# Reordering a graph layer: input normalised team by team, flips and projection placed between the products, four flip buffers

## What is computed

```python
h = relu(layernorm(x))                       # rows of 256
hidden = h @ W + b
x = x + adj @ hidden / adj.sum(axis=0)[:, None]     # layer 0
h = relu(layernorm(x))
x = x + layer1(h, S=adj)                     # two steps:
#   A = softmax of the kept 0.9 of (Xa W1 W2)(Xa W3)^T, row by row
#   Xf = Rf Xf ; Xb = Rb Xb ; Xa = A Xa  (Rf, Rb: adj + I, divided by its row and column sums)
#   Z += Xf U1 + Xb U2 + Xa U3 ; result: layernorm(X + Z) * gamma + beta
```

## Time and profile before

| what | us |
|---|---|
| median of 3 runs | 2404.68 (2404.57 to 2407.76) |
| the profiled execution's own time | 2408.84 |
| its span, first to last instruction | 2406.6 |
| start until the main products of tile 0 (L730) | 60.0 |
| first layer, tiles 0 to 25 | about 60 to 365 |
| second norm and projections, until the first logits | about 365 to 445 |
| attention layer, two steps, and the end | about 445 to 2406.6 |

### The profile page before, as it was taken

The page is one execution under the profiler, slowest core; times in us unless marked ns, Lnnn a source line. Parts: engine busy times, 40 slices in busy tenths (PEclk is TensorE's granted clock), DMA queues, the critical chain, the costliest instruction groups (busy, mean ns, idle before and its releaser), DMA issues.

```text
span 2406.6 us, 38368 instructions
## 1 busy us (share of the span) xinstructions
PE 1959.0 (81%) x12364; PEld 1462.6 (61%) x12364; DVE 1722.7 (72%) x4419; ACT 1223.4 (51%) x1886; POOL 68.3 (3%) x115
## 2 busy tenths in 40 slices
PE   0888884479999999999656498988989898898980
PEld 0777772267777777777444166665656666565660
DVE  5111116488888888888882688888888888888866
ACT  1111113556666666666331675766657576665720
POOL 0000002100000000000000000000000000000000
PEclk9999996689999999999878699999999999999995
DMA  4555551111111111111003001001010100101003
GB/s 107 142 142 142 142 127 71 32 36 40 40 40 43 43 48 46 41 43 40 19 20 97 19 18 35 25 27 35 17 35 17 35 30 22 35 17 35 16 20 118
DMA packets 59226, 123.87 MB, mean 51 GB/s; under 512 B 13491, under 2 KB 45617, under 8 KB 58928
## 3 DMA queue, kind: packets, MB, share of 16 engines
q1 hardware_dynamic: 45872, 93.58, 11.5%
q0 software_dynamic: 3744, 22.14, 5.3%
q10 hardware_dynamic: 9568, 7.67, 1.0%
HBM read 107.99 MB, written 37.49 MB: 60 GB/s over the span
## 4 chain that ended last, share of the span: by engine, by line
DVE 34%; PE 31%; DVEq 13%; ACT 12%; issue 7%; DMA 2%; ACTq 1%; SPq 0%
DVE scraps L1064 7%; PE bank L730 7%; PE bank L817 6%; DVE stats L1194 5%; DVE window L1064 4%; PE lg L783 4%; ACT turned L600 3%; ACT turned L602 3%; DVEq L1369 3%; PE bank L826 3%; ACT expo L583 3%; PE bank L849 3%; PE bank L803 3%; DVEq L1241 2%; DVE window L1237 2%
## 5 line engine op out<-in xcount | busy, mean ns | idle before, releaser
L826 PE MATMUL bank<-xcur,probs_t 128*128 128x256 f32 x2704 | 597.4, 381 | 2.5 <-ACT probs_t L636 2.5
L826 PEld LDWEIGHTS bank<-xcur,probs_t 128*128 128x128 f32 x2704 | 509.5, 190 | 76.3 <-issue 3.3
L817 PE MATMUL bank<-ident,window 128*128 128x128 f32 x1352 | 242.3, 337 | 193.4 <-DVE kept_inv L1371 172.7
L817 PEld LDWEIGHTS bank<-ident,window 128*128 128x128 f32 x1352 | 182.3, 170 | 281.4 <-DVE kept_inv L1371 196.5
L636 ACT ACTIVATE probs_t<-bank 128x512 f32<-128x512 f32 (+1 forms) x364 | 194.9, 566 | 299.6 <-PE bank L817 297.6
L803 PE MATMUL bank<-both,s_tile 128*128 128x512 f16 x1352 | 300.1, 379 | 0.0
L1049 DVE TENSOR_SCALAR_CACHE_REDUCE expo<-lg 128x1024 f32 (+1 forms) x208 | 204.9, 1022 | 122.0 <-PE lg L783 113.3
L583 ACT ACTIVATE expo<-expo,neg_max 128x3327 f32<-128x3327 f32 x52 | 159.7, 3070 | 232.3 <-DVE neg_max L1058 232.3
L602 ACT ACTIVATE turned<-expo,found 128x3327 uint8<-128x3327 f32 x78 | 239.6, 3071 | 5.4
L600 ACT ACTIVATE turned<-expo,found 128x3327 uint8<-128x3327 f32 x78 | 239.3, 3068 | 3.7
L1194 DVE MAX8 stats<-window 128x8 f32<-128x208 f32 (+1 forms) x780 | 238.8, 384 | 0.0
(11 more groups left out here) (226 smaller groups left out, 2181.4 us busy)
## 6 DMA issues: line engine op xcount, KB each, us to landing
s_tile<-s_scratch SPq DMA_DIRECT2D x52, 832.0 KB, 4.6
s_scratch<-s_tile SPq DMA_DIRECT2D x26, 832.0 KB, 3.4
expo<-in_adj POOLq DMA_DIRECT2D x25, 831.8 KB, 7.1
x_scratch<-both SPq DMA_DIRECT2D x1, 3328.0 KB, 9.5
q_tile<-q_scratch SPq DMA_DIRECT2D x104, 32.0 KB, 3.3
xa_scratch<-ht ACTq DMA_DIRECT2D x26, 128.0 KB, 1.7
y_scratch<-y_tile ACTq DMA_DIRECT2D x26, 128.0 KB, 1.7
xcur<-xa_scratch SPq DMA_DIRECT2D x1, 3328.0 KB, 12.4
```

The costliest lines, as they stand in the source:

```text
L817: last = T.transpose(flip_ps[g % 2][:, k * P:(k + 1) * P], window[:, (k0 + k) * P:(k0 + k + 1) * P], ident[:, :])
L826: last = T.matmul(pv_ps[:, 0:D], probs_t[:, k * P:(k + 1) * P], xcur[:, k, :], start=(k == 0), stop=(k == NT - 1))
```

## The change

- **Input.** `x` is loaded by team, without waiting for `x_pad` (only the tail does). For each team VectorE makes moments, reciprocal and `-mean * rstd`; ScalarE makes the square root, one Relu with scale and bias for each tile and one copy for the high part; GpSimd makes the low part, one tile at a time, after it has issued the first two `adj` loads, and signals `low_first`. TensorE waits for `low_first` team by team inside tile 0's products.
- **First layer.** Four flip buffers instead of two (the two new ones lie in `probs_t` and `window`), and two PSUM tiles for the products (`s_ps`, `lg[1]`). The counts and flips of tile t+1 stand among tile t's products, before k = 12, 14, 18 and 21; the transposes of tile t-1 stand before k = 3 and its projection before k = 8. The hardware loop has 6 passes of four tiles. VectorE's and ScalarE's moves follow that order.
- **Weights.** W1 times W2 is made after tile 0's products.
- **Second norm.** The column counts are closed before tile 25's products. VectorE starts on the inverses and on teams 0 and 1 then; its last work for tile 25 (`with_loops`, `projected_out`) and the row and column inverses stand ahead of team 2.

```diff
+TURN_AT = 3
+PROJECT_AT = 8
+FLIP_AT = (12, 14, 18, 21)
+TEAM_STARTS = [t0 for t0, _ in TEAMS]
+        s_buf = [s_tile[0], s_tile[1]] + [home[:, c0:c0 + NP // 2].bitcast(BF16).rearrange("p (k q) -> p k q", k=NT)
+                                          for home, c0 in ((probs_t, (DC + 1) * D), (window, 0))]
+        conv_ps = [s_ps, lg[1]]
+        def at(i, j):
+            return i * 4 + j, i * 2 + j // 2, j % 2, i + j // 4, j % 4
+        def convolve_all(eng, convolve):
+            convolve(at(0, 0), at(0, 1), first=True)
+            with eng.Fori(0, NT // 4) as i:
+                for j in range(1, 5):
+                    convolve(at(i, j), at(i, j + 1))
 # SyncE
+            for g, (t0, n) in enumerate(TEAMS):
+                full = min(n, NT - 1 - t0)
+                sp.dma_start(xcur[:, t0:t0 + full, :], ...).then_inc(x_in[g], DMA)
             sp.wait_ge(x_pad, 1)
-            sp.dma_start(xcur[:, 0:NT - 1, :], ...).then_inc(x_in, DMA)
 # GpSimd
-                pool.wait_ge(x_in, DMA * 2)
-            tiles_loop(pool, load_adj)
+            pool.wait_ge(x_in[NTEAM - 2], DMA)
+            for t in range(2):
+                load_adj(t, 0, t)
+            for g, (t0, n) in enumerate(TEAMS):
+                pool.wait_ge(high_first, g + 1)
+                for t in range(t0, t0 + n):
+                    last = G.tensor_tensor(parts[:, t, 1, :], x1_all[:, t, :], parts[:, t, 0, :], ALU.subtract)
+                last.then_inc(low_first, 1)
...
 # ScalarE
+            deviation_x(0)
+            for g, (t0, n) in enumerate(TEAMS):
+                if g + 1 < NTEAM:
+                    deviation_x(g + 1)
+                act.wait_ge(norm_x, g + 1)
+                for t in range(t0, t0 + n):
+                    A.activation(x1_all[:, t, :], xcur[:, t, :], ACT.Relu, scale=rstd[:, t:t + 1], bias=mean[:, t:t + 1])
+                act.drain()
+                A.activation(parts[:, t0:t0 + n, 0, :], x1_all[:, t0:t0 + n, :], ACT.Copy).then_inc(high_first, 1)
+            for g in range(1, NA, 2):
+                move_flipped(at(0, 0), g)
+            convolve_all(act, convolve)
+            convolve(at(NT // 4, 1), None)
+            turned_out(NT - 1)
 # TensorE
+            def convolve(tile, after, first=False):
+                t, _, b, _, q = tile
                 pe.wait_ge(adj_moved_v, (t + 1) * (NA // 2) + 1)
                 pe.wait_ge(adj_moved_s, (t + 1) * (NA // 2) + 1)
-                pe.wait_ge(conv_out, t + 1)
                 for k in range(NT):
+                    if first and k in TEAM_STARTS:
+                        pe.wait_ge(low_first, TEAM_STARTS.index(k) + 1)
+                    if not first and k == TURN_AT:
+                        turn_convolved(t - 1)
+                    if not first and k == PROJECT_AT:
+                        project(t - 1)
+                    if after is not None and k == FLIP_AT[0]:
+                        count_columns(after)
+                    if after is not None and k in FLIP_AT:
+                        flip(after, FLIP_AT.index(k))
...
                 last.then_inc(conv_done, 1)
+                if first:
+                    multiply_weights()
 # VectorE
-            norm_stats(xcur)
-            stds(1)
...
+            input_moments(0)
+            for g in range(NTEAM):
+                if g + 1 < NTEAM:
+                    input_moments(g + 1)
+                input_normaliser(g)
+            def convolve(tile, after, first=False):
+                if not first:
+                    projected_out(tile[0] - 1)
+                for g in range(0, NA, 2):
+                    move_flipped(after, g)
+                with_loops(tile)
 # VectorE, second norm
             for g in range(NTEAM):
+                if g == 1:
+                    with_loops(at(NT // 4, 1))
+                    projected_out(NT - 1)
+                    dve.drain()
+                    inverse_sums()
```

More of the change, by code:

```diff
@@ L299, in graph_layers @@
         free_slots = [
-            *[(s_stored[n], DMA) for n in range(2)],
+            *[(s_stored[n], DMA) for n in range(4)],
             (adj_flipped, 8),
@@ L385, in _, with store_s @@
             load_u(0)
[L388 removed]
+            def store_s(tile):
+                t, _, _, _, q = tile
                 sp.wait_ge(s_made, t + 1)
[L390 to L391 removed]
+                sp.dma_start(dram_tile(s_dram, t), flat(s_buf[q][:, :, :])).then_inc(s_stored[q], DMA)
+            with sp.Fori(0, NT // 4) as i:
+                for j in range(4):
+                    store_s(at(i, j))
+            for j in range(NT % 4):
+                store_s(at(NT // 4, j))
             sp.wait_ge(x1_ready, 1)
@@ L504, in _ @@
         def _(act):
[L505 to L528, removed]
+            def deviation_x(g):
+                t0, n = TEAMS[g]
+                act.wait_ge(moments_x, g + 1)
+                A.activation(rstd[:, t0:t0 + n], var[:, t0:t0 + n], ACT.Sqrt).then_inc(deviations_x, 1)
@@ L711, in convolve, with flip @@
                              skip_group_check=True)
[L713 to L724, removed]
+            def flip(tile, g):
+                t, _, b, _, _ = tile
+                k0, n = ADJ_GROUPS[g]
+                pe.wait_ge(adj_moved_s if g % 2 else adj_moved_v, t * (NA // 2) + g // 2 + 1)
+                view = flip_ps[g % 2][:, :].bitcast(BF16)
+                for k in range(n):
+                    last = T.transpose(view[:, k * P:(k + 1) * P], natural[b][:, (k0 + k) * P:(k0 + k + 1) * P], ident_bf[:, :])
+                last.then_inc(adj_flipped, 1)
@@ L733, in convolve @@
                                     skip_group_check=True)
                 last.then_inc(conv_done, 1)
[L736 to L740, removed]
+                if first:
+                    multiply_weights()
+            count_columns(at(0, 0))
+            for g in range(NA):
+                flip(at(0, 0), g)
@@ new lines, in convolve @@
+            def convolve(tile, after, first=False):
+                if not first:
+                    projected_out(tile[0] - 1)
+                for g in range(0, NA, 2):
+                    move_flipped(after, g)
+                with_loops(tile)
+            for g in range(0, NA, 2):
+                move_flipped(at(0, 0), g)
+            convolve_all(dve, convolve)
+            projected_out(NT - 2)
+            dve.wait_ge(cols_done, 1)
+            V.tensor_copy(col_n[:, :], lg[0][:, 0:NT])
@@ L989, in normaliser, with result_moments @@
+            def result_moments(g):
+                t0, n = TEAMS[g]
+                for t in range(t0, t0 + n):
+                    V.scalar_tensor_tensor(out=x1_all[:, t, :], in0=x1_all[:, t, :], scalar=deg_inv[:, t:t + 1], in1=xcur[:, t, :],
+                                           op0=ALU.mult, op1=ALU.add)
+                dve.drain()
+                moments_of(x1_all, g).then_inc(moments, 1)
             def normaliser(g):
```

190 lines of the change are left out of this document (104 added, 86 removed).

## The result

The changed kernel takes 2320.66 us (median of 4, 2319.51 to 2321.97), the kernel before 2405.86 (median of 4, 2404.57 to 2407.76): ratio 0.9645, 95% interval 0.9629 to 0.9662. Forecast 2322, range 2310 to 2342. The profiled execution took 2319.51, its span is 2317.8, against 2406.6 before.

The account below looks back on a forecast made before the run. TensorE paces the loop at 11.84 us a tile and does nothing that counts until 60 us. Gains of 74.3 through tile 25 and 7.9 in the second norm, 82.2, take 2408.84 to 2326.6; median 4.2 lower: forecast 2322, range 2310 to 2342.

Parts of the forecast that it names:

- Start: Input stage: products of tile 0 start at 34.2 us instead of 60.00.
- Tile 0: First tile of the first layer, from its products to tile 1's start: 12.4 us, with ten slow steps and W1 W2.
- Tile: Steady tile of the first layer's loop: 9.85 us of TensorE work instead of 11.84, for 24 tiles 236.4.
- Tile 25: Last tile of the first layer, without flips: 7.6 us, its products ending at 290.6 instead of 364.9.
- Second norm: Products' end to the second norm's first Relu: 6.2 us instead of 14.15, a gain of 7.9.
- The handshakes: Loop waits between engines: each fits into products placed over it; for the transposes three steps, 0.73 against 0.70, stall at most 0.05.
- rival 6: Loop: adj's load misses its place, taking over 21.5 us instead of 7.1; tile 13.3, gain gone; at 22 about 2410; chance 0.01.
- the longer loop's stall: Loop's jump back: TensorE waits for code, 2 us in each of six passes, 12 us in all, 2334; chance 0.08.
- Array run-out at the switches: Loop: TensorE's array empties at switches between products and other work, 1.3 us a tile, 31 in all, 2353; chance 0.07.
- The input rival: Input stage: VectorE's small operations, stretched by GpSimd, fall behind ScalarE from team 3, 6 to 10 us, about 2330; chance 0.08.

## Why the prediction came out right

Forecast and result are 1.3 us apart. The mechanism was right, and the closeness is partly luck: two errors took most of each other back.

First, the steps against the profiled execution: 82.2 predicted, 88.8 measured in the span. *Start* 34.2 predicted, 34.8 measured (by the table above it can come nearly 3 us later). *Tile 0*: its products to tile 1's, 12.4 predicted; tile 1's transposes stand at 46.72, three steps after its first product, which is 11.2. Six steps were slow (34.80 to 37.48), where the prediction took ten by the earlier trace rows: 0.9 of the 1.2. *Tile*: 9.85 predicted, 9.65 measured; 24 tiles make 4.9 of it. Each price was right in kind and a little high (counts, transposes, flips and projection 0.68, 0.3, 1.56, 0.97 against 0.65, 0.25, 1.47, 0.94), probably because I read distances between rows with small waits between them. *Tile 25*: 7.6 and 7.5. *Second norm*: 7.9 and 8.0; the run without it cost 7.7 at that place. 1.0 more came behind it: VectorE's four operations L1064 (L971 before) of team 3 took 2.07 instead of 3.11.

Second, the profiled execution before (2408.84) lies above its median, and the one after (2319.51) is the fastest of its four; so 89.3 between profiles is 85.2 between medians. The prediction used the gain from the profile, 82.2, as one between medians; there it is 3.0 too small, and the median before came out 1.2 higher with a fourth run. So the 6.6 by which the steps fell short shrank to 1.3.

The handshakes were judged rightly: two steps less for the transposes cost 0.45 a tile, one PSUM tile 0.76, and flips in a block 1.55 (the brackets of the earlier trace rows sum to 1.54, but the waits are split otherwise).

One reason in the prediction was right for a wrong cause. It said that nothing waits because a flip buffer is wanted again four tiles after its store. That is so, but I took the store for a transfer of 3.4 us and wrote before the run with two buffers that it would hardly matter. In the new order load and store overlap and both take about 9; with two buffers the whole gain of the kernel is gone and 10 more. The tile is then 13.6, close to the 13.3 at which rival 6 had put the end of the gain, but through the store and not through the load. (Rival 6's slack is misadded: two tiles of 13.3 less 4.5 are 22.1, not 21.5.) So with load and store in this order the four buffers are not a detail but a condition; with the load held behind the store two buffers still keep 62.9 of the gain.

Of the rivals, the longer loop's stall does not show: the transposes follow at 9.63 to 9.67, a tile behind a jump is at most 0.03 over the others, and 24 tiles average 9.65. The rule of the Trainium skill that the prediction cites (Runtime: NRT & Kernel Launch, "Instruction fetch mechanics") did not bite in this loop. But the prediction misread the kernel before when it said that its passes of two tiles showed no gap. The transposes there follow at 11.77 and 11.97 in turn (211.69, 223.46, 235.43, and so on through the loop), 0.20 more once in each pass, and 11.78 where the loop ends without a jump. With the transposes two steps earlier every fourth tile takes 10.17 instead of 10.09. So something at the turn of a pass costs 0.08 to 0.20 us where TensorE has no work to cover a handshake, and next to nothing where it has. Eleven such turns make about 2 us of the loop's gain; they were in the 11.84 of the prediction without a name. No run isolates the jump itself. Array run-out at the switches does not show: the sum of the prices (9.67) is the pitch. The input rival happened in small (the Relu groups at 16.97 and 21.59) and in some kernels took back up to 3 us; I had not foreseen that one operation can be held for many of GpSimd's in a row.

## What to carry to other kernels

When an in-order engine loses time to handshakes, count for each how many steps of independent work stand between issue and use, and place them by that count: here three steps of 0.2445 (0.73) covered 0.70, and one did not.

Before moving the release of a load, look which other transfer it then meets: the time to landing read from the old order does not hold in the new one, and every buffer that was sized for it has to be sized again.

A long wait for a small transfer can be an order on a queue. One store moved to another queue gave 13 us, a sixth of what the whole reordering gave.

## What the runs showed of the hardware that was not expected

- A VectorE operation on 4 numbers a partition, normally 0.17 us, was held 5.61 us while GpSimd ran twelve 128x256 subtractions of 0.66 back to back (5.59 and 4.47 in two other runs); in the two runs in which GpSimd stayed silent until VectorE had normalised all teams, none was held. That some nine of GpSimd's operations in a row can pass first, and not one, is more than the rule of the Trainium skill that the prediction cites (SBUF — State Buffer, "SBUF: two separate sides") says. A tensor_scalar on one input was held too (2.99 us, with GpSimd at work). In the changed kernel's own profile no hold was longer than 0.71.
- The load of adj and the store of a flipped tile landed in 7.1 and 3.4 us when apart, and in 8.9 and 9.1 (medians) when issued 1.1 us after each other in the changed kernel.
- The granted clock fell to 0.87 over a loop in which TensorE stood 1.7 to 4.0 us once in each tile. After a stand of 3.83 it was 0.50, and eight flips took 1.03 instead of 0.61.
- A pass of the hardware loop made one tile 0.20 us longer in the kernel before (11.97 against 11.77), and at most 0.03 in the changed one, whose handshakes are covered.
